# Zero rows written between the weight loads, the last group's side chain spread in half units, and all 24 shared-expert units ahead of the tiles

## The chip, the cores and the metric

The kernel runs on one core of a Trainium2 chip, as one program of five instruction streams: PE (TensorE), DVE (VectorE), ACT (ScalarE), POOL (GpSimd) and SP (SyncE, which here only issues DMAs). Each stream runs in its own order and the streams meet only at semaphores. The metric is the device time of one execution in microseconds; lower is better.

## The reference

Two layers of a decoder on 16 sequences of 128 tokens with 256 channels, all in float32. Each step is added to x:

```
x = x + self_attention(layernorm(x))        # 16 heads of 128
x = x + wkv(keys=layernorm(x), values=ctx)  # a scan over the 128 tokens, per channel
x = x + experts(layernorm(x))               # below
x = x + narrow_attention(layernorm(x)); x = x + cross_attention(layernorm(x), ctx); x = x + bitnet_ffn(layernorm(x))
```

The experts step picks for each token 4 of 16 experts (hidden width 176 each) and has a shared expert (hidden width 704) that all tokens go through:

```
probs = softmax(h @ router_w.T); top_vals, top_idx = top_k(probs, 4); top_vals /= top_vals.sum()
routed = sum over the picked experts of weight * (silu(h @ w_gate[e]) * (h @ w_up[e])) @ w_down[e]
shared = silu(h @ sh_gate) * (h @ sh_up) @ sh_down
out = routed + sigmoid(h @ sh_gate_w) * shared
```

## The kernel before

**Groups.** The 16 sequences of 128 tokens are 4 groups (`g` = 0 to 3) of 512 tokens. `X` ("residual") holds x, `XT` ("x_channel_major") the normalised x turned so that channels are on the partitions, as a high and a low part: a full-precision product is three matmuls (L552, L553, L554), one for each pair of parts that matters.

**Self-attention, `NSTEP` = 64 steps.** Sixteen passes `p` (a group and four of its heads), each of four steps `n` (one sequence). In pass p the PE also fills the queries, keys and values of pass p+1, three of twelve `fill`s a step. The weights of a pass come in three thirds of 512 KB. SP fetches third t (L2619) into one of two raw buffers once `w_split` has reached t-4; POOL splits it into the high part (L2401) and the low part (L2403), and the PE's first fill of a pass waits for that (`w_split`, `3 * (p - 1) + m + 1`). After the thirds SP fetches the pass's bias (L2624) and output weights `wo` (L2626), which waits until the PE's output of an earlier pass is done (`a_output`, `GB * (p - 1)`), so everything behind it in SP's queue waits for that as well.

**Zero rows.** The picked experts read their tokens from an array in HBM, `picked_inputs`, with 2048 rows for each of 16 experts (1 KB a row, 32 MB), of which each token's rows are scattered to their places and the rest has to be zero. SP writes the zeros from an SBUF tile, 34 DMAs, five behind `wo` in each pass from p = 1 on (`zero(i)`, 1 MB each, L2645), so they are through in the first seven passes. All scatters wait for all zeros.

**Side work.** Beside the main loop every engine has a list `side` of generators; `side.step()` runs the next one to its next `yield`. While attention works on group g+1, the side list holds group g's `wkv_group` (norm, two channel halves c of the scan: `wkv_chunk`), `routing` (norm, turned x, logits, top 4) and `dispatch` (rows of the picks, then `scatter`: 16 indirect DMAs of POOL, L2429). Of the wkv chunk, POOL makes two products (`wkv_helps`, L2409 and L2410) for groups 0 to 2, DVE (L1255, L1256) for group 3. Group 3 has no attention behind it: its side work runs beside the shared expert.

**Shared expert.** `UNITS` are 24 units, six hidden blocks of 128 for each group, groups in the order 0, 1, 3, 2. For a unit the PE makes two products (`up`: 12 matmuls), ACT a silu (L2135), DVE the product (L1534), ACT the high part (L2143), POOL the low part (L2491), and two units later (`LAG` = 2) the PE adds it into two banks (`down`: 6 matmuls). At the end of a group ACT copies, the PE turns (L765) and DVE adds the result into X (L1543). The weights of the six blocks are split first (`split_weights`: DVE L1526 and L1527, POOL L2485 and L2487). `NBEFORE` = 18 units (groups 0, 1, 3) come before the tiles, with three side steps after every half unit on the PE, DVE and ACT (six a unit on POOL); before the first unit of group 3, each engine steps its side list until group 3 is dispatched:

```
            for i in range(NBEFORE + LAG):
                if i < NBEFORE:
                    while UNITS[i][0] == NG - 1 and NG - 1 not in done:
                        side.step()
                    up(i)
                side.step(3)
```

The PE's turning of the wkv result (L597, waiting for `wkv_y`) stands in that order about as many side steps after the chunk's start as DVE needs side steps to make it.

**Tiles.** After `make_tables` and the last scatter, 79 tiles (`NTILE`) of 128 picked rows go through their expert: SP fetches (L2705) and stores (L2709), the PE turns, multiplies (L793, L802, L810, L819). Then come the six units of group 2. Beside them POOL gathers the results of group 0 back, four indirect DMAs for each sequence (`gather`, L2451), and DVE weighs and adds them (`combine`, L1554). Then `second_norm(0)` (DVE L1165 to L1182, PE L564) begins the narrow attention.

## Time and profile before

| | us |
|---|---|
| median of 3 runs | 1977.72 (1971.71 to 1977.88) |
| the profiled execution, time | 1987.48 |
| its span, first to last instruction | 1985.7 |
| attention, with groups 0 to 2 beside it | 0 to 701.6 |
| 18 shared units, with group 3's chain | 701.6 to 880.0 |
| 79 tiles | 880.0 to 1079.4 |
| last 6 units, first combine and norm | 1079.4 to 1121.0 |
| narrow attention, cross attention, bitnet | 1121.0 to 1985.7 |

Times in the trace are microseconds from the span's start. A row of the timeline gives start, duration, engine, line, operation and operands; in brackets stands how long the engine was idle before it and what ended that. PEclk is the clock granted to TensorE as a share of full speed. A DMA's row stands in the queue of the engine that issues it (SPq) and shows when it was issued, not when it landed.

### The profile page before, as it was taken

How to read it: one execution, taken by the hardware profiler on the slowest of the kernel's cores; microseconds unless marked ns; L12 is line 12 of the kernel's file. 1: busy time of each engine (PE TensorE's matmuls, PEld its weight loads, DVE VectorE, ACT ScalarE, POOL GpSimd, SP SyncE). 2: the span in 40 equal slices, each digit the busy share in tenths (PEclk: the TensorE clock that was granted, in tenths of full speed). 3: DMA queues.
4: the chain of work that ended last, by engine and by line, in shares of the span. 5: the costliest groups of instructions: out<-in, count | busy, mean ns of one | idle time of the engine just before them, and what ended most of it. 6: DMA issues, size and time to landing. Idle time of an engine off the chain costs nothing. (4 is left out here: it accounts for less than half of the span.)

```text
span 1985.7 us, 25633 instructions
## 1 busy us (share of the span) xinstructions
PE 1656.2 (83%) x8566; PEld 1319.4 (66%) x8566; DVE 1233.1 (62%) x2690; ACT 870.7 (44%) x2514; POOL 545.3 (27%) x442
## 2 busy tenths in 40 slices
PE   6977788987988744779999668789887999999866
PEld 5866677876877633557777446667665888788644
DVE  4643367577657736425443556766665778877878
ACT  4533334443443322312223134456434666666756
POOL 2222232362253051230001455545113122311000
PEclk9988889998999876989999757989889999999989
DMA  7255442231121024223332311100101110000001
GB/s 272 103 190 181 156 168 96 87 110 48 59 91 54 22 101 117 66 67 106 104 108 88 115 33 33 32 11 1 43 1 40 28 48 27 31 1 1 1 1 43
DMA packets 81414, 143.23 MB, mean 72 GB/s; under 512 B 8452, under 2 KB 43780, under 8 KB 81156
## 3 DMA queue, kind: packets, MB, share of 16 engines
q1 hardware_dynamic: 75140, 124.81, 19.2%
q0 software_dynamic: 6144, 16.79, 2.6%
q8 instruction: 70, 1.15, 0.2%
q14 instruction: 60, 0.49, 0.1%
HBM read 86.90 MB, written 54.66 MB: 71 GB/s over the span
## 5 line engine op out<-in xcount | busy, mean ns | idle before, releaser
L552 PE MATMUL bank<-x_channel_major,qkv_weights_split 128*128 128x512 f32 x256 | 120.1, 469 | 48.3 <-POOL qkv_weights_split L2403 43.3
L2082 ACT ACTIVATE self_attention<-self_attention,small 128x128 f32<-128x128 f32 x256 | 100.0, 392 | 116.4 <-DVE small L1446 115.5
L703 PE MATMUL bank<-self_attention 128*128 128x256 f32 x512 | 134.6, 410 | 17.0 <-DVE residual L1465 14.0
L2586 POOL TENSOR_TENSOR cross_attention_heads<-cross_attention_heads 128x512 f32<-128x512 f32 x64 | 70.4, 1100 | 285.3 <-DVE cross_attention_heads L1798 285.2
L2298 ACT ACTIVATE cross_attention_heads<-cross_attention_heads,small 128x128 f32<-128x128 f32 x256 | 99.6, 390 | 90.3 <-DVE small L1822 90.3
L2214 ACT ACTIVATE narrow_attention<-bank,small 128x128 f32<-128x128 f32 x256 | 90.4, 365 | 108.2 <-DVE small L1688 103.5
L1048 PE MATMUL bank<-cross_attention,cross_attention_heads 128*128 128x256 f32 x512 | 124.4, 386 | 15.0 <-DVE residual L1836 10.2
L703 PEld LDWEIGHTS bank<-self_attention 128*128 128x128 f32 x512 | 104.9, 209 | 38.2 <-DVE residual L1465 17.7
L2451 POOL DMA_INDIRECT narrow_attention<-picked_outputs,dispatch x64 | 62.6, 977 | 242.0 <-DMA picked_outputs<-tiles 208.4
L2401 POOL CAST qkv_weights_split<-self_attention 128x1024 fp32r<-128x1024 f32 x45 | 48.9, 1087 | 289.6 <-DMA self_attention<-in_wqkv 252.7
L1048 PEld LDWEIGHTS bank<-cross_attention,cross_attention_heads 128*128 128x128 f32 x512 | 95.2, 190 | 38.2 <-DVE residual L1836 22.4
L2403 POOL TENSOR_TENSOR qkv_weights_split<-self_attention,qkv_weights_split 128x1024 fp32r<-128x1024 f32 x45 | 108.7, 2416 | 3.6
L802 PE MATMUL bank<-experts,tiles 128*128 x316 | 108.0, 465 | 0.4 <-DVE tiles L1580 0.4
L553 PE MATMUL bank<-x_channel_major,qkv_weights_split 128*128 128x512 f32 x256 | 105.1, 410 | 0.0
L554 PE MATMUL bank<-x_channel_major,qkv_weights_split 128*128 128x512 f32 x256 | 104.8, 409 | 0.0
L1437 DVE TENSOR_TENSOR self_attention<-bank,self_attention 128x512 f32<-128x512 f32 x64 | 43.7, 684 | 92.5 <-PE bank L554 80.1
L2090 ACT COPY self_attention<-bank 128x512 f32<-128x512 f32 x64 | 37.4, 585 | 144.7 <-PE bank L684 123.9
L904 PE MATMUL bank<-narrow_attention 128*128 128x16 f32 x512 | 70.3, 271 | 25.1 <-DVE narrow_attention L1693 14.4
L552 PEld LDWEIGHTS bank<-x_channel_major,qkv_weights_split 128*128 128x128 f32 x256 | 50.6, 198 | 59.7 <-POOL qkv_weights_split L2403 44.5
L1458 DVE COPY self_attention<-bank 128x512 f32<-128x512 f32 x64 | 43.7, 683 | 74.4 <-PE bank L693 74.3
L904 PEld LDWEIGHTS bank<-narrow_attention 128*128 128x128 f32 x512 | 69.6, 211 | 28.8 <-DVE narrow_attention L1693 27.9
L2429 POOL DMA_INDIRECT picked_inputs<-normalised_tiles,dispatch x64 | 62.3, 974 | 90.1 <-DVE dispatch L1386 71.9
(363 smaller groups left out, 4689.7 us busy)
## 6 DMA issues: line engine op xcount, KB each, us to landing
picked_inputs<-self_attention SPq DMA_DIRECT2D x32, 1024.0 KB, 10.4
self_attention<-in_wqkv SPq DMA_DIRECT2D x48, 512.0 KB
experts_far<-picked_inputs SPq DMA_DIRECT2D x79, 128.0 KB, 2.1
picked_outputs<-tiles SPq DMA_DIRECT2D x79, 128.0 KB, 1.7
self_attention<-in_wo SPq DMA_DIRECT2D x16, 512.0 KB, 4.0
experts<-in_moe SPq DMA_DIRECT2D x4, 1408.0 KB, 12.6
self_attention<-in_bv SPq DMA_DIRECT2D x16, 256.0 KB, 4.1
bitnet_weights<-in_bitgu SPq DMA_DIRECT2D x8, 416.0 KB, 3.4
```

What stands on the lines that cost most here:

```text
L552: T.matmul(out_ap, w_hi, x_hi, start=first, stop=False)
L553: T.matmul(out_ap, w_hi, x_lo, start=False, stop=False)
L554: return T.matmul(out_ap, w_lo, x_hi, start=False, stop=last)
L703: m = T.matmul(bank[7][:, 0:D], ZT_a[n % 2][:, h, :], wo_a[p % 2][:, h, :], start=h == 0, stop=h == HG - 1)
L802: m = T.matmul(bank[2 + n % 2][:, 0:2 * EI].rearrange("p (m c) -> p m c", m=2), t_xT[n % 2][:, k, :], wup[:, :, k, bass.ds(at, EI)], start ...
L904: m = T.matmul(bank[6][:, hh * DS:(hh + 1) * DS], n_PT[n % 2][:, h, :], n_v[bb % 8][:, hh * DS:(hh + 1) * DS], start=True, stop=True)
L1048: m = T.matmul(bank[7][:, 0:D], ZT_x[n % 2][:, h, :], x_wo[hg % 2][:, h, :], start=h == 0, stop=h == HG - 1)
L2082: m = S.activation(P_a[u][:, h, :], P_a[u][:, h, :], ACT.Exp, bias=negmax_a[u][:, h:h + 1], accum_out=sums_a[u][:, h:h + 1])
L2214: m = S.activation(n_P[v][:, h, :], s4_in[:, h, :], ACT.Exp, bias=n_negmax[v][:, h:h + 1], accum_out=n_sums[bb % 2][:, q4 * 4 + h:q4 * 4 + ...
L2298: m = S.activation(P_x[u][:, h, :], P_x[u][:, h, :], ACT.Exp, bias=negmax_x[u][:, h:h + 1], accum_out=sums_x[u][:, h:h + 1])
L2403: G.tensor_tensor(wqkv[m][1], third(t), wqkv[m][0].bitcast(F32), ALU.subtract).then_inc(w_split, 1)
L2586: G.tensor_tensor(x_qsq, x_queries[f % 2], x_queries[f % 2], ALU.mult).then_inc(x_squared, 1)
```

## The change

1. The zeros are 64 DMAs of 512 KB (one for each expert and group) and three small ones. SP writes one behind each third, in all passes, and one or two behind `wo`. A scatter of group g waits only for the zeros of groups up to g (two semaphores in turns).
2. The weight split of the shared expert moves from DVE to ACT and, with POOL's part, into the last steps of attention (blocks 0 to 3 at n = 63 to 66; 4 and 5 in units 1 and 2). The loads of blocks 2 to 5 are issued earlier.
3. Units go in the order 0, 1, 2, 3 and all 24 stand ahead of the tiles. Between half units each engine takes one side step. Group 3's chain is one generator for each engine, `last_group`, with its pauses written by hand. POOL makes the wkv products for group 3 as well. Group 2's scatters move from the end of attention into it, four at a time between units.
4. From unit `DVE_UNIT` = 15 on, DVE makes the low part instead of POOL, whose queue then has group 3's 16 scatters.
5. Behind the tiles no units are left: all four `combine`s and `second_norm(0)` follow at once.

```diff
-SHARED = [0, 1, 3, 2]
+SHARED = [0, 1, 2, 3]
 UNITS = [(g, j, j == 0, j == NSH - 1) for g in SHARED for j in range(NSH)]
 NUNIT = len(UNITS)
-NBEFORE = NUNIT - NSH
...
+            def last_group():
+
+                c, g = KT * (NG - 1), NG - 1
+                yield from pause(3)
+                last_keys(c)
+                yield from pause(5)
+                last_keys(c + 1)
+                yield from pause(5)
+                last_y(c)
+                yield from pause(5)
+                last_y(c + 1)
+                yield from pause(4)
+                turn_xt(NORM["routing", g], 0)
...
-            for i in range(NBEFORE + LAG):
-                if i < NBEFORE:
-                    while UNITS[i][0] == NG - 1 and NG - 1 not in done:
-                        side.step()
+            for i in range(NUNIT + LAG):
+                if i < NUNIT:
                     up(i)
-                side.step(3)
+                side.step()
                 if i >= LAG:
                     down(i - LAG)
-                side.step(3)
+                side.step()
             side.finish()
...
             pe.wait_ge(tables_set, 1)
-            pe.wait_ge(e_added, KT * (NG - 1))
+            pe.wait_ge(e_added, KT * NG)
...
             pe.wait_ge(t_outs, NTILE)
-            for i in range(NBEFORE, NUNIT + LAG):
-                if i < NUNIT:
-                    up(i)
-                if i >= NBEFORE + LAG:
-                    down(i - LAG)
             side.add(second_norm(0))
...
+            def last_group():
+                yield
+                scatter(NG - 2, 0)
+                yield from pause(3)
+                scatter(NG - 2, 1)
+                yield from pause(2)
+                wkv_helps(KT * (NG - 1))
...
+            for i in range(NUNIT + LAG):
+                if i in (1, 2):
+                    split_weights(i + 3)
+                if i < DVE_UNIT:
                     up(i)
-                side.step(6)
+                side.step(2)
...
+                g, e = divmod(i, E)
+                if i == 2 * E:
+                    sp.wait_ge(*all_zeroed(0))
+                if i == 3 * E:
+                    sp.wait_ge(*all_zeroed(1))
+                at = e * NT + g * GT
+                to = picked_x[at:at + GT, :].rearrange("(p a r) d -> p a (r d)", p=P, a=2)
+                D_(to, zero_a.unsqueeze(1).broadcast_to([P, 2, 512])).then_inc(zeroed[g % 2], 16)
...
             for p in range(1, NHG * NG):
+                first, end = (q * NG * E // (NHG * NG - 1) for q in (p - 1, p))
                 for m in range(3):
                     fetch_third(3 * p + m)
+                    zero(first + m)
                 fetch_output(p)
-                for i in range(5 * (p - 1), min(5 * p, E * NT // ZERO_ROWS + 2)):
+                for i in range(first + 3, end):
                     zero(i)
```

The order on SP's queue, attention pass 1 (thirds, bias, `wo`, zeros) and the start of pass 2; `in_wqkv` are thirds, `picked_inputs<-self_attention` zeros. Before:

```order
L2619 DMA self_attention<-in_wqkv 128x1024 x3
L2624 DMA self_attention<-in_bv 128x512
L2626 DMA self_attention<-in_wo 128x1024
L2645 DMA picked_inputs<-self_attention 512x1x512 x5
L2619 DMA self_attention<-in_wqkv 128x1024 x3
L2624 DMA self_attention<-in_bv 128x512
L2626 DMA self_attention<-in_wo 128x1024
L2645 DMA picked_inputs<-self_attention 512x1x512 x5
```

and now:

```order
L2848 DMA self_attention<-in_wqkv 128x1024
L2877 DMA picked_inputs<-self_attention 256x1x512
L2848 DMA self_attention<-in_wqkv 128x1024
L2877 DMA picked_inputs<-self_attention 256x1x512
L2848 DMA self_attention<-in_wqkv 128x1024
L2877 DMA picked_inputs<-self_attention 256x1x512
L2853 DMA self_attention<-in_bv 128x512
L2855 DMA self_attention<-in_wo 128x1024
L2877 DMA picked_inputs<-self_attention 256x1x512
L2848 DMA self_attention<-in_wqkv 128x1024
```

Behind `wo` five 1 MB zeros have become one of 512 KB, and one stands behind each third.

The order on POOL where attention ends and the shared expert begins; `first_weights` and `experts` with 128x512 and 128x256 are the weights' low parts, then 128x512 alone is a unit's. Before:

```order
L2409 TENSOR_TENSOR wkv<-wkv 128x4x128
L2410 TENSOR_TENSOR wkv<-wkv 128x512
L2429 DMA picked_inputs<-normalised_tiles,dispatch 33024x256 x16
L2485 TENSOR_TENSOR experts_split<-first_weights,experts_split 128x512
L2487 TENSOR_TENSOR experts_split<-first_weights,experts_split 128x256
L2485 TENSOR_TENSOR experts_split<-first_weights,experts_split 128x512
L2487 TENSOR_TENSOR experts_split<-first_weights,experts_split 128x256
L2485 TENSOR_TENSOR experts_split<-experts,experts_split 128x512
L2487 TENSOR_TENSOR experts_split<-experts,experts_split 128x256
L2491 TENSOR_TENSOR experts_split<-experts,experts_split 128x512
L2485 TENSOR_TENSOR experts_split<-experts,experts_split 128x512
L2487 TENSOR_TENSOR experts_split<-experts,experts_split 128x256
```

and now:

```order
L2625 TENSOR_TENSOR wkv<-wkv 128x4x128
L2626 TENSOR_TENSOR wkv<-wkv 128x512
L2686 TENSOR_TENSOR experts_split<-first_weights,experts_split 128x512
L2688 TENSOR_TENSOR experts_split<-first_weights,experts_split 128x256
L2686 TENSOR_TENSOR experts_split<-first_weights,experts_split 128x512
L2688 TENSOR_TENSOR experts_split<-first_weights,experts_split 128x256
L2686 TENSOR_TENSOR experts_split<-experts,experts_split 128x512
L2688 TENSOR_TENSOR experts_split<-experts,experts_split 128x256
L2686 TENSOR_TENSOR experts_split<-experts,experts_split 128x512
L2688 TENSOR_TENSOR experts_split<-experts,experts_split 128x256
L2723 TENSOR_TENSOR experts_split<-experts,experts_split 128x512
L2645 DMA picked_inputs<-normalised_tiles,dispatch 33024x256 x4
```

Group 2's 16 scatters no longer stand ahead of the first weights; they come in fours between the first units.

The order on DVE inside the first wkv chunk of group 3; `experts<-experts,bank` is the unit's product, of which the others wait. Before:

```order
L1258 SCALAR_TENSOR_TENSOR wkv<-wkv 128x516
L1261 TENSOR_TENSOR wkv<-wkv 128x512
L1263 TENSOR_TENSOR wkv<-wkv 128x512
L1268 SCALAR_TENSOR_TENSOR wkv<-wkv 128x516
L1273 RECIPROCAL wkv<-wkv 128x256 x2
L1526 CAST experts_split<-experts 128x512
L1527 CAST experts_split<-experts 128x256
L1534 TENSOR_TENSOR experts<-experts,bank 128x512
L1276 TENSOR_TENSOR wkv<-wkv 128x512
L1282 TENSOR_TENSOR wkv<-wkv 128x512
L1285 TENSOR_TENSOR wkv<-wkv 128x512
L1290 TENSOR_TENSOR residual<-bank,residual 128x4x128
```

and now:

```order
L1512 SCALAR_TENSOR_TENSOR wkv<-wkv 128x516
L1517 TENSOR_TENSOR wkv<-wkv 128x512
L1519 TENSOR_TENSOR wkv<-wkv 128x512
L1523 SCALAR_TENSOR_TENSOR wkv<-wkv 128x516
L1710 TENSOR_TENSOR experts<-experts,bank 128x512
L1528 RECIPROCAL wkv<-wkv 128x256 x2
L1532 TENSOR_TENSOR wkv<-wkv 128x512
L1535 TENSOR_TENSOR wkv<-wkv 128x512
L1537 TENSOR_TENSOR wkv<-wkv 128x512
L1710 TENSOR_TENSOR experts<-experts,bank 128x512
L1494 SCALAR_TENSOR_TENSOR wkv<-wkv 128x516
L1499 SCALAR_TENSOR_TENSOR wkv<-wkv,wkv_decay 128x4x128
```

The casts of the weights are gone from between, and less of the chunk stands between two units' products.

## Rows read from the trace of the kernel before

**Rows 1.** Busy time by stretch: start:end, length, five engines, clock, DMA share, GB/s.

```profile
0.00:701.60 701.60, 584.53 (x3093) 496.21 (x3093) 429.18 (x839) 280.78 (x793) 215.53 (x151) 0.93 0.34 116
701.60:880.00 178.40, 101.19 (x391) 77.30 (x391) 78.20 (x176) 45.62 (x69) 63.89 (x59) 0.80 0.31 90
880.00:1079.40 199.40, 198.91 (x948) 146.74 (x948) 91.56 (x257) 54.08 (x158) 0.00 (x0) 0.99 0.33 101
1079.40:1121.00 41.60, 28.33 (x117) 21.72 (x117) 20.48 (x47) 10.22 (x17) 24.11 (x24) 0.90 0.34 97
1121.00:1985.70 864.70, 743.25 (x4018) 577.42 (x4018) 613.72 (x1372) 479.96 (x1478) 241.74 (x208) 0.91 0.08 25
```

**Rows 2.** Waits of the PE from 90 to 300 us: total, times, longest.

```profile
PE bank L552 <- POOL qkv_weights_split L2403: 43.3, 5, 10.8
```

**Rows 3.** Timeline of SP's queue, POOL and PE in one pass with zeros.

```profile
133.42 0.33 SPq L2626 DMA_DIRECT2D self_attention<-in_wo  x1
133.79 6.29 SPq L2645 DMA_DIRECT2D picked_inputs<-self_attention  x5
...
153.08 1.04 POOL L2401 CAST qkv_weights_split<-self_attention 128x1024 fp32r<-128x1024 f32 x1 [34.65 <-DMA self_attention<-in_wqkv]
...
156.59 0.79 PE L552 MATMUL bank<-x_channel_major,qkv_weights_split 128*128 128x512 f32 x1 [10.04 <-POOL qkv_weights_split L2403]
...
178.23 0.33 SPq L2626 DMA_DIRECT2D self_attention<-in_wo  x1
```

**Rows 4.** The same in passes without zeros.

```profile
359.53 0.33 SPq L2626 DMA_DIRECT2D self_attention<-in_wo  x1
359.90 0.91 SPq L2631 DMA_DIRECT2D wkv<-in_ctxT  x2
...
368.15 1.04 POOL L2401 CAST qkv_weights_split<-self_attention 128x1024 fp32r<-128x1024 f32 x1 [29.10 <-DMA self_attention<-in_wqkv]
...
393.68 0.33 SPq L2626 DMA_DIRECT2D self_attention<-in_wo  x1
...
476.86 0.33 SPq L2626 DMA_DIRECT2D self_attention<-in_wo  x1
...
481.85 1.04 POOL L2401 CAST qkv_weights_split<-self_attention 128x1024 fp32r<-128x1024 f32 x1 [5.95 <-DMA self_attention<-in_wqkv]
```

**Rows 5.** Waits of the PE from 701.6 to 880.1 us, the two largest.

```profile
PE bank L597 <- DVE wkv L1285: 31.5, 2, 17.1
PE bank L552 <- POOL experts_split L2485: 17.6, 1, 17.6
```

**Rows 6.** Stretches as in Rows 1: one wkv chunk, and two undisturbed units.

```profile
768.70:790.20 21.50, 7.15 (x31) 5.44 (x29) 18.02 (x19) 7.20 (x10) 3.74 (x3) 0.73 0.57 138
1089.69:1098.06 8.37, 8.37 (x38) 6.75 (x37) 3.92 (x7) 2.44 (x4) 6.24 (x8) 1.00 0.34 100
```

**Rows 7.** Groups of DVE instructions, 701.6 to 880 us: busy, mean ns, idle before.

```profile
L1534 DVE TENSOR_TENSOR experts<-experts,bank 128x512 f32<-128x512 f32 x18 | 12.3, 684 | 66.5 <-PE bank L554 46.5 <-ACT experts L2135 14.8 <-issue 5.2
...
L1543 DVE SCALAR_TENSOR_TENSOR residual<-bank,small,residual 128x128 f32<-128x128 f32 x24 | 6.8, 344 | 11.6 <-PE bank L765 7.4 <-issue 3.9
```

**Rows 8.** One DVE line over the whole run: ns shortest/median/longest.

```profile
L1453 DVE TENSOR_TENSOR self_attention<-self_attention,small x64: 691/693/2389, 44.4 to 690.3; 128x512 f32<-128x512 f32 x64
```

**Rows 9.** Timeline: last scatter and first tile fetch; first and sixteenth gather.

```profile
857.77 0.96 POOL L2429 DMA_INDIRECT picked_inputs<-normalised_tiles,dispatch  x1 [0.30 <-issue]
...
861.42 1.88 SPq L2705 DMA_DIRECT2D experts_far<-picked_inputs  x4
...
1082.25 0.98 POOL L2451 DMA_INDIRECT narrow_attention<-picked_outputs,dispatch  x1 [208.37 <-DMA picked_outputs<-tiles]
...
1101.79 0.95 POOL L2451 DMA_INDIRECT narrow_attention<-picked_outputs,dispatch  x1 [0.30 <-issue]
```

**Rows 10.** Timeline: last adds of `combine` for group 0, and the norm's first turn.

```profile
1116.46 1.53 DVE L1554 SCALAR_TENSOR_TENSOR residual<-narrow_attention,dispatch,residual 128x256 f32<-128x256 f32 x3
...
1120.98 0.71 PE L564 MATMUL bank<-identity,normalised_tiles 128*128 128x128 f32 x2 [6.92 <-DVE normalised_tiles L1182]
```

492 lines of the change are left out of this document (335 added, 157 removed).

## Prediction

> **What bounds the kernel now.** I read the stretches first [rows 1], then the PE's waits in each, then the queues behind the longest waits. The PE is busy 198.9 of 199.4 us in the tiles and 743 of 865 us behind them; the change touches neither. It touches three stretches: attention (701.6 us, PE busy 584.5), the 18 shared units with group 3's chain (178.4 us, busy 101.2, at a mean granted clock of 0.80) and the 41.6 us behind the tiles.
>
> In attention 43.3 us are five waits for the first third of a pass [rows 2]. One of them in the queues [rows 3]: SP issues `wo` at 133.42, then five 1 MB zeros, then the thirds; POOL, idle for 34.65 us for lack of a third, begins its cast at 153.08, 19.7 us after `wo`. Cast and subtraction take 3.5 us and end the PE's wait of 10.04 us. Without zeros the cast begins 5.0 us after `wo`, and 8.6 us after it where two 256 KB values are fetched in between [rows 4]. So 5 MB of zeros cost 14.7 us, 1.5 us for each 512 KB, and 512 KB of values cost 3.6 us. `wo` follows `wo` after 44.8 us with zeros [rows 3] and 34.2 us without [rows 4].
>
> In the second stretch two turns of the wkv result hold the PE for 31.5 us, and the first weights for 17.6 us [rows 5]. Where nothing disturbs them a unit takes 8.37 / 2 = 4.2 us [rows 6]; here 178.4 us went by for 18.
>
> **Part 1, zeros.** The same bytes are written, but `wo` has one zero of 512 KB behind it, in passes 4, 8, 12 and 15 two. How late may a third land? The PE went idle at 156.59 - 10.04 = 146.55; less 3.5 us for cast and subtraction, less 133.42: 9.6 us after `wo` [rows 3]. By the zeros' price it now lands after 5.0 + 1.5 = 6.5 us, with two zeros after 7.9 us: in time. In passes 8 and 12, where values are fetched too, after 8.6 + 2.9 = 11.5 us: 1.9 us late. The zeros between the thirds delay the second and third by 1.5 us each, hidden by POOL's 3.5 us for each third. Four passes go from 44.8 to 34.2 us: 42.6 us. Of the fifth wait 43.3 - 4 x 10.04 = 3.1 us are left, since group 0's wkv begins there and loads DVE. Less 2.5 us for each late pass: 42.6 + 3.1 - 5 = **41 us gained**. Bounds: 50 if no pass is late and the clock that fell in the stalls comes back whole; 34 if the zeros cost what the values cost (two passes 6.3 us late, two 2.6 us, so 13 more than I take, less what POOL's and DVE's queues hide). I take the zeros' own row. The two added waits on zeros are for DMAs issued more than three passes earlier, and cost nothing. The three small zeros ahead of pass 1's thirds are 384 KB, 1.1 us, where POOL and PE still work on pass 0.
>
> **Part 2, first weights.** Group 2's 16 scatters no longer stand before the split on POOL, and the split is done in attention's last steps. The 17.6 us wait goes; the PE follows from its last output product. ACT has four casts more in those steps; the tail there waits on DVE, so I cost them at nothing, at most 2 us. I count this in part 3.
>
> **Part 3, the front: 24 units and the chain.** The PE's own work: 24 x 4.18 = 100.4 us, and the chain's matmuls and turns. Before, 391 matmuls less 18 x 18 for the units are 67 others [rows 1]; at 0.21 to 0.26 us each (101.2 / 391, with and without the low clock) 14 to 17 us; I take 15. Sum 115 us.
>
> Who is late instead? DVE, in the first nine units. One wkv chunk keeps it busy for 18.0 us in 21.5, of which two unit products (0.68 each) and two wkv products that POOL now makes (0.68 each) do not belong to it [rows 6, 7]: 15.3 us. Twice is 30.6; norm and one add about 4 (estimate), nine unit products 6.2, eight group adds of 0.34 2.8 [rows 7], waits for ACT's exponentials inside about 5 (before, 3.5 us idle a chunk, [rows 6]): 49 us, and it begins 4 us after the PE. The PE needs 9 x 4.18 + 4 = 42 us for the same. Of the 11 us the lag of two units hides about 3: 8 us. POOL: 15 low parts of 1.25 us (3.74 / 3, [rows 6]), 16 scatters at 1.26 a piece (20 us; the gathers' pitch in [rows 9] is (1101.79 - 1082.25) / 15 = 1.30), four products, two splits: about 50 of 70 us. A block of four scatters takes 5 us; a low part is wanted some 9 us after its `up` (about two units, [rows 6]) and ACT, DVE and POOL need about 3.3 for it (estimate), so it nearly fits. For these blocks and for ACT's waits later in the chain I take 5 us. Closing (copy, turn, eight adds, first tile): 5 us, as it was. Front: 115 + 8 + 5 + 5 = 133 us, against 178.4: **45 us gained**. Group 3's scatters start at unit 15, some 50 us before the end, take 20 us and land 2.7 us later (858.73 to 861.42, [rows 9]); they and the expert weights' loads are covered. Bounds: 58 with no overhang (115 + 5), 17 by the second rival.
>
> **Part 4, the rear.** The six units go; what is late next is the gather. It starts at 1082.25 as now and sixteen are issued by 1101.79 + 0.95 = 1102.74 [rows 9]. No row shows their landing; scatter to fetch took 2.7 us, and I take that. Four adds of 0.51 us, then 3.0 us from the last add to the norm's first turn (1117.99 to 1120.98) [rows 10]: 1102.7 + 2.7 + 2.0 + 3.0 = 1110.5 instead of 1121.0: **10.5 us gained**, 8 to 12. Combines 0 to 2 fit between the gathers (2 us of work every 5).
>
> **Sum.** 41 + 45 + 10.5 = 96.5 us. The profiled execution's span of 1985.7 becomes 1889.2, its time of 1987.5 becomes 1891.0. That execution lies 9.8 us above the median of the runs, so by the median 1977.7 - 96.5 = **1881 us**.
>
> **Rivals.**
> First, attention finds its next limit: the passes with zeros may need the 44.8 us for another reason that the wait hid. For it: later passes with wkv beside them also have DVE waits. Against it: the 34.2 us of [rows 4], the same work. Only 10 of the 41 us would come: 65.5 us, 1912.
>
> Second, DVE and POOL hold each other up. DVE's L1453 takes 0.69 us, but 2.39 at worst [rows 8], so something does block it at times, and the change puts POOL's four products, scatters and low parts beside a DVE that is the late engine. If DVE waited for all of POOL's elementwise work in the first 15 units, 15 x 1.25 + 4 x 2.4 = 28 us (the four products priced at the longest L1453), the front would gain 17: 1909.
> The Trainium skill, "SBUF — State Buffer", section "Who interferes with whom", says that a Vector instruction with two SBUF inputs and a GpSimd one that reads SBUF contend, and that the one that starts second is blocked for the other's whole instruction. By that rule this rival's 28 us is the ceiling; the median of L1453, 0.69 against 2.39, says that it is met seldom.
>
> Third, slower: lock step. Each half unit now carries one hand-placed step of the chain on four engines, each in order; if every step waits for the slowest, the pace of the unit is the chain's. Before, it was (178.4 - 17.6) / 18 = 8.9 us a unit [rows 1, 5]. At 10 us, 24 units and 5 us of closing are 245 us: 66.6 lost against 51.5 gained elsewhere, 1993 us. It decides from (178.4 + 51.5 - 5) / 24 = 9.4 us a unit. Against it: the chain is finite and is over by unit 17, and DVE's whole work before was 78 of 178 us.
>
> Fourth, all is hidden: 50 + 58 + 12 = 120 us, 1858.
>
> That the change would not do what it says: the units' order and the zeros' places are as described in the built order; only the effect is open.
>
> **Chances.** Forecast 0.70; attention's next limit 0.08; blocking on the port 0.13; all hidden 0.06; slower 0.03. The range 1859 to 1912 takes the bounds of parts 1 to 4 (not all at their bad end at once) and the first two rivals at their edge; about 0.2 is left out. A measurement of this kernel tells 0.3% (6 us) from no change: faster 0.96, within it 0.01, slower 0.03.
>
> **What would show it.** Right: the PE's waits for the weights' low part gone between 90 and 300 us, passes of 34 us there, attention ending near 660; the first shared unit at once behind it; DVE near full in the first nine units and units of 4.2 us from the tenth on; first tile near 794; 31 us from the last tile to the norm's turn. Wrong: waits for thirds in every pass; units of 6 us or more behind unit 15; a tile stage longer than 199.4 us, or a clock below what it was behind the tiles, which nothing here foresees.

## The result, and the profile after

The changed kernel takes **1910.7 us** (median of 4 runs, 1909.7 to 1912.2) against 1976.9 us of the kernel before on the same chip: ratio 0.967, 95% interval 0.965 to 0.969. That is 66 us less; 96.5 were forecast. The time lies at the upper edge of the range of 1859 to 1912.

The stretches of the changed kernel, to be held against [rows 1] (columns: window, its length, then busy time and instructions of PE, weight loads, DVE, ACT and POOL, granted clock, DMA share, GB/s):

```profile
0.00:667.70 667.70, 580.70 (x3094) 493.69 (x3095) 452.37 (x839) 283.36 (x801) 220.71 (x156) 0.95 0.37 125
667.70:814.70 147.00, 118.92 (x508) 92.00 (x507) 88.07 (x183) 58.12 (x89) 63.28 (x55) 0.94 0.33 97
814.70:1014.70 200.00, 199.81 (x948) 147.17 (x948) 91.69 (x257) 54.06 (x157) 0.00 (x0) 0.99 0.33 101
1014.70:1044.70 30.00, 0.03 (x1) 0.06 (x1) 10.32 (x27) 1.95 (x3) 20.71 (x22) 0.56 0.65 210
1044.70:1908.60 863.90, 740.19 (x4018) 575.27 (x4018) 612.90 (x1372) 479.93 (x1478) 244.40 (x211) 0.92 0.07 22
```

Attention ends at 667.7 instead of 701.6, the 24 units and the chain take 147.0 us where 18 took 178.5, the tiles are unchanged, the rear (from the last tile's copy to the norm's first turn) takes 29.9 us instead of 41.6. One number stands out: in attention DVE is busy for 452.4 us with 839 instructions; before, the same 839 took 429.2 [rows 1].

The PE's waits, first in attention (to 660 us), then in the front, that is, the 24 units with group 3's chain (columns: what waited for what, us in total, times, longest). [rows 2] had five waits for POOL's low part in attention, 43.3 us; two are left, 2.1 us, in passes 8 and 12:

```profile
PE bank L606 <- DVE wkv L1325: 22.8, 3, 8.6
PE bank L561 <- DVE self_attention L1618: 16.1, 4, 5.2
PE bank L573 <- DVE normalised_tiles L1230: 16.0, 7, 8.8
PE bank L757 <- DVE residual L1646: 9.7, 7, 4.8
...
PE bank L561 <- POOL qkv_weights_split L2619: 2.1, 2, 1.1
```

```profile
PE bank L819 <- ACT experts L2371: 13.0, 4, 8.1
PE bank L660 <- DVE wkv L1537: 4.4, 2, 2.4
PE bank L573 <- DVE normalised_tiles L1230: 3.6, 1, 3.6
PE bank L846 <- DVE residual L1719: 2.6, 1, 2.6
PE bank L561 <- POOL experts_split L2723: 1.9, 2, 1.5
PE bank L573 <- DVE x_channel_major L1237: 1.1, 1, 1.1
PE bank L561 <- DVE experts L1710: 1.0, 1, 1.0
```

L819 is the turn of a finished group's sums: the PE stops there until ACT has copied them out of PSUM. In attention nearly everything that is left is a wait for DVE: 78.9 of 84 us to 660 us. Before, the PE's waits for DVE there were 59.6 us.

### The profile page after: what moved, and what is told of

It reads as the page before. It is cut to its first block and busy times, and to the rows that moved or that the text cites. A ratio compares the mean times of both kernels' runs of the same rounds, so it can differ in the third digit from the quotient of the medians.

```text
span 1908.6 us, 25684 instructions
## 1 busy us (share of the span) xinstructions
PE 1639.6 (86%) x8566; PEld 1308.2 (69%) x8566; DVE 1255.4 (66%) x2677; ACT 877.4 (46%) x2528; POOL 549.1 (29%) x443
## 5 line engine op out<-in xcount | busy, mean ns | idle before, releaser
L757 PE MATMUL bank<-self_attention 128*128 128x256 f32 x512 | 132.0, 404 | 12.5 <-DVE residual L1646 12.5
L1096 PE MATMUL bank<-cross_attention,cross_attention_heads 128*128 128x256 f32 x512 | 124.2, 385 | 14.9 <-DVE residual L2001 10.1
L561 PE MATMUL bank<-x_channel_major,qkv_weights_split 128*128 128x512 f32 x256 | 118.8, 464 | 7.2 <-DVE qkv_weights_split L1664 2.9
L757 PEld LDWEIGHTS bank<-self_attention 128*128 128x128 f32 x512 | 102.5, 204 | 32.0 <-DVE residual L1646 15.5
L1096 PEld LDWEIGHTS bank<-cross_attention,cross_attention_heads 128*128 128x128 f32 x512 | 95.1, 190 | 38.1 <-DVE residual L2001 22.3
L573 PE MATMUL bank<-identity,normalised_tiles 128*128 128x128 f32 x160 | 36.6, 333 | 80.2 <-DVE normalised_tiles L1230 57.4
L562 PE MATMUL bank<-x_channel_major,qkv_weights_split 128*128 128x512 f32 x256 | 103.8, 406 | 0.0
L563 PE MATMUL bank<-x_channel_major,qkv_weights_split 128*128 128x512 f32 x256 | 103.8, 405 | 0.0
L573 PEld LDWEIGHTS bank<-identity,normalised_tiles 128*128 128x128 f32 x160 | 22.7, 159 | 97.8 <-issue 61.6
L1070 PEld LDWEIGHTS bank<-cross_attention,cross_attention_heads 128*128 128x128 f32 x512 | 66.7, 192 | 27.0 <-issue 26.8
```

What stands on the lines that cost most here:

```text
L561: T.matmul(out_ap, w_hi, x_hi, start=first, stop=False)
L562: T.matmul(out_ap, w_hi, x_lo, start=False, stop=False)
L563: return T.matmul(out_ap, w_lo, x_hi, start=False, stop=last)
L757: m = T.matmul(bank[7][:, 0:D], ZT_a[n % 2][:, h, :], wo_a[p % 2][:, h, :], start=h == 0, stop=h == HG - 1)
L1070: m = T.matmul(bank[2 + n % 2][:, h * P:(h + 1) * P], x_qT[p % 2][:, h, ts], x_kT[:, g * GB + b, hg, :], start=True, stop=True)
L1096: m = T.matmul(bank[7][:, 0:D], ZT_x[n % 2][:, h, :], x_wo[hg % 2][:, h, :], start=h == 0, stop=h == HG - 1)
```

## The experiments

Each set of kernels ran on one chip beside the kernel before, which took 1976.9 us in set 0 and 1975, 1989, 1984 and 1974 us in sets 1 to 4. Between sets I therefore compare ratios to before; within a set, times. Only sets 0 and 3 hold the unaltered changed kernel. The ratios of set 2 run low: attention and front of later_scan end at 814.9 us, those of the changed kernel at 814.7, yet the ratios are 0.962 and 0.967. A difference of 0.005 between sets (10 us) shows nothing without the stage lengths beside it. Stage lengths are from the one profiled execution of each kernel: attention to the PE's last output product, the front from there to the first turn of the tiles (L846).

| kernel | set | median us | ratio to before (95%) | attention | front |
|---|---|---|---|---|---|
| changed | 0 | 1910.7 | 0.967 (0.965 to 0.969) | 667.7 | 147.0 |
| zeros_alone | 1 | 1942.6 | 0.983 (0.981 to 0.985) | 666.6 | 176.2 |
| open_later | 1 | 1901.7 | 0.963 (0.960 to 0.965) | 658.8 | 148.1 |
| wkv_on_dve | 1 | 1907.2 | 0.965 (0.963 to 0.967) | 665.6 | 146.3 |
| finish_first | 1 | 1912.6 | 0.968 (0.966 to 0.970) | 667.6 | 150.7 |
| later_scan | 2 | 1912.4 | 0.962 (0.960 to 0.964) | 670.7 | 144.2 |
| halved_low | 2 | 1910.5 | 0.961 (0.958 to 0.963) | 658.4 | 157.6 |
| later_turn | 2 | 1905.5 | 0.958 (0.956 to 0.961) | 654.1 | 155.9 |
| no_scatter | 2 | 1919.9 | 0.965 (0.962 to 0.969) | 671.9 | 151.5 |
| changed_again | 3 | 1922.2 | 0.969 (0.967 to 0.972) | 666.6 | 153.6 |
| all_four | 3 | 1883.5 | 0.950 (0.948 to 0.953) | 641.8 | 144.2 |
| low_on_dve | 3 | 1922.9 | 0.970 (0.967 to 0.972) | 667.1 | 159.5 |
| all_five | 4 | 1882.5 | 0.953 (0.951 to 0.956) | 641.1 | 143.9 |

Three theories stand against each other. A: DVE and POOL hold each other up, since a removed stall brings POOL's work beside DVE's (the forecast's second rival, but in attention too); a hold-up is a DVE instruction that lasts until one of POOL is over. B: DVE simply has too much to do (first rival). C: the order of a queue turns one late product into an idle PE.

### Part 1 by itself

```diff
 # the kernel before, with zero(), zeroed[2] and the places of the zeros of the changed kernel;
 # group 3's value products count on DVE's own semaphore to free one
+                    fetch_third(3 * p + m)
+                    zero(first + m)
...
-                for i in range(5 * (p - 1), min(5 * p, E * NT // ZERO_ROWS + 2)):
-                    zero(i)
```

> The kernel before with the new placing of the zeros and nothing else. The trace of the changed kernel ends attention 34 us earlier than the trace of before. If the zeros alone did that, attention ends at about 667 here too and the time is 1977 - 34 = 1943. The prediction's own term (41 us) would give 1936. If part of the 34 us came from the other parts (scatters and splits that moved), the time stays above 1948. In each case the PE's waits for the weights' low part between 90 and 300 us are down to about 2 us.

32.5 us less by the medians (1975.2 to 1942.6), and attention ends at 666.6, as in the changed kernel. So the zeros give 32.5, the other parts 66.2 - 32.5 = 34 us; forecast were 41 and 55.5. Attention's shortfall is in the kernel without any of the other parts, and so is DVE's longer busy time:

```profile
0.00:666.60 666.60, 580.33 (x3093) 493.30 (x3093) 452.09 (x839) 280.22 (x793) 215.83 (x151) 0.95 0.36 122
```

The two profiles would say more than 32.5 us: 35.0 less in attention, 2.3 in the front, 6.7 in the rear. The profile of the kernel before holds waits with no cause in the profile in all three stages (last section).

### Where 7.6 us of attention stayed

The pass that begins at 88.2 took 41.0 us, not the 34.2 of a pass without zeros [rows 4]; it has one wait, for DVE's add into the residual (L1646). In front of this late add DVE opens the wkv state, 12 small instructions, and two of them are long. First the wait and POOL's and DVE's rows in the changed kernel (columns: start, duration, instruction, in brackets the idle time and its releaser):

```profile
100.45 2.37 POOL L2619 TENSOR_TENSOR qkv_weights_split<-self_attention,qkv_weights_split 128x1024 fp32r<-128x1024 f32 x1
104.88 2.42 POOL L2619 TENSOR_TENSOR qkv_weights_split<-self_attention,qkv_weights_split 128x1024 fp32r<-128x1024 f32 x1
101.09 1.75 DVE L1267 TENSOR_SCALAR wkv_decay<-wkv_decay 128x2 f32<-128x2 f32 x1
105.31 2.07 DVE L1675 TENSOR_SCALAR dispatch<-self_attention 128x128 bf16<-128x128 f32 x1
108.37 3.78 PE L757 MATMUL bank<-self_attention 128*128 128x256 f32 x8 [4.75 <-DVE residual L1646]
```

and the same two in the kernel before, where POOL waited for the third at that time:

```profile
101.26 0.16 DVE L1219 TENSOR_SCALAR wkv_decay<-wkv_decay 128x2 f32<-128x2 f32 x1
103.89 0.23 DVE L1494 TENSOR_SCALAR dispatch<-self_attention 128x128 bf16<-128x128 f32 x1
```

In the changed kernel both last until the subtraction on POOL is over: 101.09 + 1.75 = 102.84 against 100.45 + 2.37 = 102.82; 105.31 + 2.07 = 107.38 against 107.30. The Trainium skill, "SBUF — State Buffer", section "Who interferes with whom", says that `tensor_scalar` on DVE can run in a mode that takes the port pair it shares with GpSimd, and that whoever issues first has the pair for the whole instruction while the other is blocked. The trace agrees, to 0.1 us.

These two are not alone. In attention of the changed kernel 45 more DVE instructions last over 0.15 us longer than the shortest of their kind. Each overlaps an elementwise instruction of POOL and ends behind its end by no more than about its own ordinary length. With the two, DVE loses 55 us in this way. In the kernel before it was 35 instructions and 35 us.

```diff
-                if n == 8:
+                if n == 9:
                     wkv_open()
```

> The changed kernel with the 12 small DVE instructions that open the wkv state one step later (step 9 instead of 8), when POOL's queue holds no split of weights. Theory A, DVE and POOL hold each other up: at step 8 two of these instructions took 1.75 and 2.07 us instead of 0.16 and 0.23, each until a 2.4 us subtraction on POOL was over. Then they are short here, the PE's 4.8 us wait in that pass (for the residual's add) shrinks by about 3.4 us or goes, and the kernel takes 3 to 5 us less, about 1906. Theory B, it is the amount of DVE work in that pass: the wait moves by one step, keeps 3 us or more, and the time stays within 2 us of 1910.7.

9 us less than the changed kernel by ratio (0.963 against 0.967), and attention ends 8.9 us earlier; that is twice what A foresaw. The wait is gone (no PE wait at all between 88 and 121 us) and the pass takes 33.4 us. L1267 is still held up there (1.66 us), which A had not expected, but nothing waits behind it: the opening now stands behind the add. A good part of the rest is the clock. After the wait the changed kernel (first row) computed at a granted clock of 0.50, 1.2 GHz, where open_later (second row) keeps 1.00, 2.4 GHz:

```profile
108.40:113.10 4.70, 4.70 (x11) 3.79 (x12) 2.58 (x4) 2.22 (x9) 0.00 (x0) 0.50 0.02 3
```

```profile
108.40:121.30 12.90, 12.90 (x75) 11.35 (x74) 7.80 (x22) 7.58 (x23) 0.00 (x0) 1.00 0.00 1
```

41.0 - 33.4 = 7.6 us for a wait of 4.75. Of the 2.9 on top, 2.4 are the clock. The same eleven matmuls, eight of L757 and one each of L561, L562 and L563, stand at 94.88 in the same trace, and the next one begins after 2.43 us; behind the wait it begins after 4.86 (108.37 to 113.23):

```profile
94.88 1.89 PE L757 MATMUL bank<-self_attention 128*128 128x256 f32 x8
97.31 0.39 PE L561 MATMUL bank<-qkv_weights_split,x_channel_major 128*128 128x512 f32 x1
113.23 0.56 PE L561 MATMUL bank<-x_channel_major,qkv_weights_split 128*128 128x512 f32 x1
```

B is out for this pass, since the same instructions one step later cost nothing. How much of the wait is hold-up and how much only the place of the opening, this run can't tell; the next one can.

### Smaller pieces on POOL

```diff
-                G.tensor_tensor(wqkv[m][1], third(t), wqkv[m][0].bitcast(F32), ALU.subtract).then_inc(w_split, 1)
+                for k in range(KT):
+                    last = G.tensor_tensor(wqkv[m][1][:, k], third(t)[:, k], wqkv[m][0][:, k].bitcast(F32), ALU.subtract)
+                last.then_inc(w_split, 1)
```

> The changed kernel with POOL's 2.4 us subtraction of each third's low part as two of half the width. Nothing else moves. If a DVE instruction that meets a POOL one stands until that one is over (theory A), then the longest stand is 1.2 us instead of 2.4: the two small instructions at step 8 take under 1.4 us each instead of 1.75 and 2.07, DVE's busy time in attention falls from 452 by 5 to 12 us (it was 429 before the change, for the same 839 instructions), and the time falls by 2 to 4 us. If DVE gets the port back only when POOL's queue is empty, both halves are waited for, and nothing changes.

DVE's busy time in attention falls from 452.4 to 432.8 us, nearly to the 429 of before, and attention is 12 to 14 us shorter than in the two kernels of the same set that don't touch it (658.4 against 670.7 and 671.9; 9 us shorter than the changed kernel's 667.7). L1267 takes 0.33 us and ends at 100.62, just when POOL's first half, begun at 99.33, is over (2.52 / 2 = 1.26): DVE does get in between the halves.

```profile
0.00:658.40 658.40, 576.15 (x3094) 490.31 (x3095) 432.81 (x839) 283.11 (x801) 233.11 (x201) 0.96 0.38 127
```

```profile
99.33 2.52 POOL L2620 TENSOR_TENSOR qkv_weights_split<-self_attention,qkv_weights_split 128x512 fp32r<-128x512 f32 x2
100.29 0.33 DVE L1267 TENSOR_SCALAR wkv_decay<-wkv_decay 128x2 f32<-128x2 f32 x1
105.76 2.61 PE L757 MATMUL bank<-self_attention 128*128 128x256 f32 x8 [2.95 <-DVE residual L1646]
```

This run shows the cause in the pass at 88 us. The opening takes 2.8 us in the kernel before, 6.2 in the changed one and 4.4 here: 1.8 us of hold-up are gone, and the PE's wait is 1.8 us shorter (2.95 against 4.75). So 3.4 of the 4.75 us were hold-up, and the other 1.3 the place of the opening in front of the add.

By ratio (0.961 against 0.967) the whole kernel takes 12 us less, but set 2's ratios run low, and beside later_scan, which has another edit, it is 2 us. In its profile the front is 10 us longer than the changed kernel's, for a reason that belongs to the run (below).

### Is DVE late, or is the PE early?

```diff
-                yield from pause(15)
+                yield from pause(18)
                 pe.wait_ge(wkv_y, c + 1)
...
 # DVE, ACT and POOL: three steps more at the end of each chunk of groups 0 to 2
```

> The changed kernel with each wkv chunk of the first three groups three steps longer, and the PE's turn of its result three steps later. In attention the PE waits 22.8 us for three of these results before 660 us, in the changed kernel as in the one before. If the PE is only early there (the place of the turn is at fault), a step is some 2 us and these waits fall to 5 us or less: attention 10 to 18 us shorter, about 1896. If DVE is late with all it does, the wait turns up at the next DVE product (the line of the queries' and keys' copies) and the time stays within 3 us. This is the rival 'attention's next limit' measured from the other side.

Attention takes 654.1 us, 17 less than in the two kernels of the set that leave it alone and 13.6 less than in the changed kernel; ratio 0.958. The time, 1905.5 us, is 7 us under later_scan's beside it. The three waits of 22.8 us for L1325 are gone, and 12 of them come back as waits for DVE's product L1617 (before: 16.1, 4 times):

```profile
PE bank L561 <- DVE self_attention L1617: 28.3, 7, 5.3
```

So the PE stood too early at half of them, and DVE is late for the rest. Attention's next limit is DVE. But these waits were there before the change too (20.2 us, 3 times), so they are room for another change and explain only 2.6 us of what is missing from this one.

### The front: hold-up, amount or order

In the changed kernel, at the first group's end (712.7 to 720.8):

```profile
713.94 5.10 DVE L1512 TENSOR_TENSOR_SCAN wkv<-wkv 128x516 f32<-128x516 f32 x1 [1.07 <-ACT wkv L2237]
714.31 1.28 POOL L2723 TENSOR_TENSOR experts_split<-experts,experts_split 128x512 fp32r<-128x512 f32 x1
715.53 1.19 POOL L2625 TENSOR_TENSOR wkv<-wkv 128x512 f32<-128x512 f32 x1
716.66 1.27 POOL L2626 TENSOR_TENSOR wkv<-wkv 128x512 f32<-128x512 f32 x1
718.96 0.66 DVE L1710 TENSOR_TENSOR experts<-experts,bank 128x512 f32<-128x512 f32 x1
719.65 0.62 ACT L2364 CAST experts_split<-experts 128x512 fp32r<-128x512 f32 x1 [2.79 <-DVE experts L1710]
720.17 1.07 ACT L2371 COPY experts<-bank 128x512 f32<-128x512 f32 x2
720.80 1.97 PE L819 MATMUL bank<-identity,experts 128*128 128x128 f32 x8 [8.14 <-ACT experts L2371]
```

The scan (1.22 us elsewhere) ends 1.1 us after POOL's third instruction; unit 7's product stands behind it, ACT's cast behind that, and the copies for which the PE waits behind the cast. Five kernels take this apart.

```diff
 # wkv_on_dve: DVE, at the head of last_num; POOL's two wkv_helps of last_group go
+                V.tensor_tensor(e2v[:, :, now], e2b[:, :, now], w_value[c % 2], ALU.mult)
+                V.tensor_tensor(w_t2, w_e2, w_value[c % 2], ALU.mult).then_inc(dve.own, dve.tick())
```

> The changed kernel with the last group's four products by the value on DVE again (0.69 us each) instead of POOL. Theory A (hold-ups): the scan of 5.10 us at 713.9 takes 1.22 us, the PE's 8.1 us wait at the first group's end falls by 2 to 4 us, and the time falls by 0 to 4 us although DVE has 2.8 us more to do. Theory B (DVE's amount of work sets the first nine units): the front gets 2 to 4 us longer, about 1914.

The scan takes 2.76 us, the wait 6.1, the front 146.3 against 147.0. The scan was expected at 1.22; POOL's low part is still beside it, and the 2.3 us that it is shorter are about the two POOL instructions that are gone (1.19 + 1.27). 1907.2 us; 2 of the 3.5 us less are in attention, which the edit does not touch. What the hold-up gives back pays for DVE's extra work, no more.

```diff
 # finish_first: ACT
             for i in range(NUNIT + LAG):
+                if i >= LAG and UNITS[i - LAG][3]:
+                    finish(i - LAG)
                 if i < NUNIT:
                     up(i)
...
-                if i >= LAG and UNITS[i - LAG][3]:
-                    finish(i - LAG)
```

> The changed kernel with ACT copying a finished group's sums out of PSUM before it takes the next unit's silu and cast, instead of behind them. The PE waited 8.1, 2.9, 1.3 and 0.7 us for these copies, and at the first group's end ACT stood behind unit 7, whose product DVE had not made because of the 5.1 us scan. Theory C, the order of ACT's queue is what turns one late DVE product into an idle PE: the first wait falls by about 5 us, the sum of the four by 6 to 8, and the time by 4 to 8 us, to 1903 to 1907. Theory A or B alone: the same product is missing two units later, the PE waits there instead, and the time stays within 2 us.

C alone falls: 1912.6 us, and a front of 150.7 us. The PE's wait for the copies is halved, and the other half stands behind it as a wait for DVE's eight adds, which are behind the same scan:

```profile
PE bank L819 <- ACT experts L2371: 6.4, 4, 4.4
PE bank L561 <- DVE residual L1719: 5.8, 5, 4.0
```

```diff
 # later_scan: DVE; the later steps of last_group two (ACT's logits three) half units later on every engine
-                last_den(c + 1)
                 yield
                 last_add(c)
-                last_sum(c + 1)
-                last_num(c + 1)
+                yield
+                last_den(c + 1)
+                last_sum(c + 1)
+                yield
+                last_num(c + 1)
                 yield
```

> The changed kernel with DVE's second scan of the last group two half units later, behind unit 7's product and the first group's adds; what follows of the chain is later by two half units on each engine too. With the value products still on POOL. Theory A, the scan was held up by POOL's three instructions (5.10 us instead of 1.22) and held unit 7's product, behind which ACT's copies of the first group's sums stood: moved behind, it meets no POOL work, takes 1.2 us, the PE's 8.1 us wait at the first group's end falls to 3 or less and the adds are not late either (the run with ACT's copies first still waited 4.0 us for them). The front is 4 to 6 us shorter, about 1905. Theory B, DVE has simply too much to do up to there: the adds or unit 8's product come late instead, and the front stays within 2 us.

The scan takes 1.22 us now and the adds follow at once, yet the wait is 6.1 us, not 3: unit 7's silu stands behind ACT's two pairs of exponentials and two table loads (714.53 to 719.33), so the product comes at 719.96:

```profile
719.96 0.69 DVE L1712 TENSOR_TENSOR experts<-experts,bank 128x512 f32<-128x512 f32 x1 [4.02 <-ACT experts L2361]
```

That is 49.2 us behind the end of this kernel's attention (670.7). In the changed kernel it was 51.3 us (718.96 - 667.7), so it comes 2 us earlier, and the wait is 2 us shorter. The same holds in wkv_on_dve (49.3 us, wait 6.1): of the 3.9 us by which the scan was held up, 2 reached the PE, since ACT's silu is next. Front 144.2 us, 2.8 less. Next, the same with both queues in the new order, on top of the attention edits (all_five, below).

The fourth has all low parts of the units on DVE.

```diff
-DVE_UNIT = 15
+DVE_UNIT = 0
```

> The changed kernel with all 24 units' low parts on DVE (15 of them were on POOL). POOL then has only the scatters, two weight splits and four products in the front. If hold-ups by POOL are what makes DVE late in the first nine units, DVE gains about 5 us there and pays 9 x 0.69 = 6 us: no change within 2 us. If DVE's amount of work decides, the first nine units take 6 us more and the time is 5 to 7 us longer than the changed kernel's beside it.

1922.9 us beside 1922.2 of the unaltered changed kernel: nothing by the medians, as A has it and B does not. DVE has 15 low parts more in the front, 10.4 us at 0.69, but is busy only 3.3 us more (91.4 against 88.1), so 7 us of hold-up are gone. The profiled front is 6 us longer (159.5 to 153.6) at a granted clock of 0.90. But changed_again's profile is of its fastest run, 7.6 us under its median, and this one's is the median run, so the two fronts do not compare.

The fifth leaves out group 2's sixteen scatters.

```diff
 # POOL, last_group: without scatter(NG - 2, 0) ... scatter(NG - 2, 3); waits on their count lowered
```

> The changed kernel without group 2's sixteen scatters of picked rows, so that the experts' tiles compute on zeros there. POOL has 20 us less between 673 and 714. The prediction took 5 us for POOL's blocks of scatters and ACT's waits. If low parts that stand behind scatters matter, the PE's waits for L2723 (1.9 us) go, and, since POOL's products for the value come 3 us earlier, the first group's wait falls too: 3 to 5 us less. If only DVE's lateness counts, under 2 us less.

The ratio is 0.965 (0.962 to 0.969), no measurable gain. POOL is busy 15 us less in the front, the PE's waits for L2723 fall from 1.9 to 0.3 us, the first group's end from 8.1 to 6.2. Here no elementwise instruction of POOL stands beside the scan, which takes 1.23 us; the product of unit 7 waits for ACT's silu again, as in wkv_on_dve and later_scan. By these two waits the scatters cost 3.5 us, against 5 forecast for them and ACT; the medians can't show so little.

### The unaltered kernel once more, and all edits together

> The changed kernel once more, unaltered, beside the next two, because the kernel before took 1975 us in the first set of runs and 1989 in the second. If the two sets differ by the chip they ran on, this kernel has the same ratio to before as at first, 0.967, whatever its own time. If what was seen only in the second set (ACT and DVE idle 4 to 7 us with no releaser while group 3's sixteen scatters are on their way, and a PE wait of 7 to 9 us at the third group's end instead of 1.3) belongs to the run and not to the edits, it can turn up here too, and then accounts for 5 to 7 us.

Ratio 0.969 against 0.967, within the intervals. The profiled front is 153.6 us, where it was 147.0, with not one instruction moved: 1.6 us more at the first group's end, 3.1 at the third's (4.38 instead of 1.25), the rest spread over the stage. At the third group's end ACT takes a cast 2.8 us after its DVE product (787.65 + 0.69) is there, and the profile knows no releaser:

```profile
787.65 0.69 DVE L1710 TENSOR_TENSOR experts<-experts,bank 128x512 f32<-128x512 f32 x1 [2.44 <-PE bank L563]
791.17 0.62 ACT L2364 CAST experts_split<-experts 128x512 fp32r<-128x512 f32 x1 [5.37 <-remote]
792.33 1.97 PE L819 MATMUL bank<-identity,experts 128*128 128x128 f32 x8 [4.38 <-ACT experts L2371]
```

In halved_low, later_turn and no_scatter the wait at that place was 8.6, 7.7 and 6.9 us. Taken off down to 1.3, their fronts are 150, 149.5 and 146.

all_four is the sum of open_later, halved_low, later_turn and later_scan.

> The changed kernel with four edits at once: the opening of the wkv state at step 9, POOL's subtraction in halves, the PE's turn of a wkv result three steps later (first three groups), and DVE's second scan of the last group behind unit 7. By the traces attention got 9, 9 to 12, 14 to 17 us shorter by the first three alone and the front 3 us by the fourth. If each wait is its own, some 25 to 30 us go: ratio to the changed kernel about 0.985, 1882. If all of them are the same DVE lateness seen in different places, the largest alone is what they give together: 15 us, 1896.

1883.5 us beside 1922.2, 39 us less, and 5% less than the kernel before: more than the 25 to 30 of separate waits. With set 0's ratio for the changed kernel (0.967) it would be 33, so how much more stays open. Attention ends at 641.8, 25 us earlier; DVE is busy 428 us there, what it was before the zeros moved. What is left:

```profile
PE bank L561 <- DVE self_attention L1619: 22.2, 7, 4.8
PE bank L573 <- DVE normalised_tiles L1230: 11.5, 3, 8.6
PE bank L561 <- POOL qkv_weights_split L2621: 9.8, 4, 4.4
```

The wait for thirds, 2.1 us in the changed kernel, is 9.8: shorter passes meet the DMAs again.

```diff
 # all_five: all_four, and on ACT and DVE alike
+                if i >= LAG and UNITS[i - LAG][3]:
+                    finish(i - LAG)
                 if i < NUNIT:
                     up(i)
```

> The kernel with the four edits, and in addition ACT copies a finished group's sums and DVE adds them before either takes the next unit. With the four edits the PE still waited 7.7, 1.3, 1.3 and 0.7 us for these copies (693.21 the first): ACT had its two pairs of exponentials with two table loads and the next unit's silu and cast in front of them, 685.9 to 692.7, and DVE had its second scan out of the way already. Theory C in its full form: the order of two queues is what is left of that wait. The copies can start at about 689.4 instead of 692.6, so the first wait falls to 4.5 or less, the others below 0.7, nothing new appears behind them (with ACT's order alone, the PE waited 4.0 us for DVE's adds), and the front takes 141 to 143 us instead of 145.5: about 0.2% of the time, in the stage rather than in the medians. If the PE waits as long as before for the adds or for unit 7's product, the chain on DVE is the limit and the order gives nothing.

The first wait is 4.35 us, the others 0.68, as expected. But the wait for the wkv result grows from 3.6 to 5.8 us in sum and the front ends at 143.9 us instead of 144.2. 1882.5 us, ratio 0.953, which the intervals do not tell from all_four's 0.950. The order moves the wait; the chain on DVE, with ACT's exponentials inside, is what lasts.

## Why the prediction was right, and where 30 us went

**Part 1: right in mechanism, 8.5 us too much.** 41 forecast, 32.5 measured alone, below the part's own lower bound of 34. The waits for thirds went from 43.3 to 2.1 us, and passes 8 and 12 are late by 1.0 and 1.1, not 1.9 with 2.5 of cost. The step that failed is "four passes go from 44.8 to 34.2". Three did, and better (32.6, 33.3 and 33.8 us); the first took 41.0. In all the four passes gained 39.0 us of 42.6. Behind them the changed kernel lost 5.3 us to the one before, where 1.9 were forecast (5 for late thirds less 3.1), although its thirds are hardly late: the PE's waits for DVE are what grew. I had read the 9.6 us of slack from a stalled pass and looked for what is late next among DMAs, while it was DVE, and 3.4 us of its lateness came from POOL's work now running beside it. [rows 8] had the sign, one L1453 of 2.39 us against 0.69. The prediction took the median of 0.69 to mean that hold-ups are rare, but 17 of the 64 were held up already in the kernel before. And I gave that rival a place in the front only. It was in attention for 23 us of DVE's time, and the first pass alone lost 7.6 us by it and by the place of the opening. (A slip in the part's lower bound: the late passes there sum to 14 us more, not 13.)

**Part 2 held.** The first unit starts at 667.33, within the last output product, and ACT's four casts cost nothing that can be seen: attention ends at 666.6 without them and 667.7 with them.

**Part 3: 45 forecast, 29 measured** (zeros_alone's 176.2 to 147.0). The PE's own work is 118.9 us, not 115. In 13.4 of them the granted clock was 0.50, which accounts for more than the 4 us; at full clock the estimate was high enough. The overhang of DVE in the first nine units was put at 8: waits for norm, wkv result, x's low part and products sum to 3.6 + 4.4 + 1.1 + 1.0 = 10.1. POOL's blocks: 1.9, not 5 with ACT's waits. The term that was mis-sized is the closing, 5 us forecast: the PE's waits for the copies and the last adds are 13.0 + 2.6 = 15.6 us, and with them the stage is accounted for (118.9 + 10.1 + 1.9 + 15.6 + 0.3). I counted it once, "as it was". Every group ends with the same stop of the PE for ACT's copies, and with all engines close behind one another it is 8.1 + 2.9 + 1.3 + 0.7 us. Before, three of these ends lay in the same stretch with 4.8 us of waits (2.85, 1.25 and 0.68); the last lay behind the tiles. So the new part is the first end above all. I should have followed one group's end through ACT's queue: silu and cast of the next unit, exponentials and table loads stand in front of the copies. The 8.1 us are hold-up (2, by later_scan, wkv_on_dve and no_scatter), queue order (all_five: 3.3, of which 2 come back) and the chain.

**Part 4: 11.7 us between the two profiles, 5.0 against zeros_alone.** It looks right (10.5 forecast), but that is luck: its base was one execution's, not the kernel's. In zeros_alone the same code takes 34.9 us from the last tile's copy (1042.01) to the norm's turn (1076.92); in the profile of before, 41.6. Most of the difference is one wait on ACT between the gathers, 7.26 us without a releaser, against 2.24 in zeros_alone:

```profile
1105.15 0.62 ACT L2143 CAST experts_split<-experts 128x512 fp32r<-128x512 f32 x1 [7.26 <-remote]
```

```profile
1065.11 0.62 ACT L2145 CAST experts_split<-experts 128x512 fp32r<-128x512 f32 x1 [2.24 <-PE bank L558]
1076.92 1.35 PE L568 MATMUL bank<-identity,normalised_tiles 128*128 128x128 f32 x4 [6.92 <-DVE normalised_tiles L1186]
```

34.9 to 29.9 is 5.0 us, below the part's lower bound of 8. The gather's start, its pitch and the 3.0 us to the turn came as forecast; the last adds begin 1.9 us after the last gather's end (2.7 taken):

```profile
1039.63 2.05 DVE L1730 SCALAR_TENSOR_TENSOR residual<-narrow_attention,dispatch,residual 128x256 f32<-128x256 f32 x4 [3.12 <-DMA narrow_attention<-picked_outputs,dispatch]
1044.67 1.36 PE L573 MATMUL bank<-identity,normalised_tiles 128*128 128x128 f32 x4 [29.98 <-DVE normalised_tiles L1230]
```

**The sum.** 32.5 + 29.2 + 5.0 = 66.7, measured 66.2 (the first is of medians, the other two of single profiles). Missing from 96.5: 8.5 in attention, 16 in the front, 5.5 in the rear. The profiled execution lay 9.8 us above the median. I carried that offset along as if it lay in stages that the change leaves alone, but the rear alone was 6.7 us longer in it than in zeros_alone. That the offset came from there is likely, not shown. Two of the three parts lie below their own lower bounds; the time lies within the range because the range was drawn out to the first two rivals.

**The rivals.** The second (DVE and POOL) is true as a mechanism; it named 1909, close to the result, but by 28 us in the front, where the PE lost 2 or 3 to it: that it comes close is luck. The first is true in that DVE is the next limit in attention; it took 8.5 us there, not 31. Lock step did not happen: from 770 us on units run at 4.2 us apart from the group ends (between 735 and 770, where I had expected it from the tenth on, the chain's turns still lie between them).

## What to carry to other kernels

When a stall of one engine goes, look at who will run at that time and was not running then: here POOL's 2.4 us subtractions moved beside DVE's steps, and a DVE instruction of 0.2 us became one of 2. Keep the pieces of the engine that holds the other up small, and its partner's small preparations at a step where nothing waits behind them. And price a stage from an execution whose waits all have a releaser; a wait without one may not be the kernel's.

## What the runs showed of the hardware

- A PE wait of 4.75 us cost 7.6: the granted clock was 0.50 for the 4.7 us behind it, and 2.4 us went by that. It was 1.00 there without the wait.
- A DVE instruction with one small input (128x2) waits out a POOL subtraction to within 0.1 us. The scan at 713.94 waited for three POOL instructions in a row, although the first of them begins 0.37 us after it in the records; between two halves of one subtraction DVE got in, and in attention it got in between L2625 and L2626 (L1305 at 230.12 lasted 1.50 us; L2626 then lasted 1.74 instead of 1.27, as if POOL were held up in turn). Why the scan didn't, no run settles.
- In some executions ACT and DVE sit idle with nothing that the profile names, while scatters or gathers of POOL are on their way: ACT at 1105.15 in the profile of before, at 791.17 in changed_again, not at the same code in the first profile of the changed kernel (wait at the third group's end 1.3). It is not in the edits. In attention it goes up to 13.6 us (later_scan) and stands in the profile of before too, for DVE and ACT alike:

```profile
567.98 0.69 DVE L1437 TENSOR_TENSOR self_attention<-bank,self_attention 128x512 f32<-128x512 f32 x1 [12.40 <-remote]
```

The profiles of sets 2 and 3 show it (all_four's least, 2 us); those of sets 1 and 4, and of the changed kernel in set 0, show nothing of the kind in attention or rear. What it is stays open; no kernel was made for it.
